# A graph kernel's gather passes: the order of their first steps, and when two blocks of table work are done

## The reference

```
h = x
for _ in range(2):                                   # two message passes
    e = concat(h[src], h[dst], edge_attr)            # 288 numbers an edge
    m = relu(e @ We1 + be1) @ We2 + be2
    h = h + segment_sum(m, dst)                      # sum over a node's incoming edges
x = layernorm(x + h + bias)
# then one graph convolution; each node also gets a further loop edge to itself, with w = 1
deg = segment_sum(w, dst);  dinv = 1/sqrt(deg), 0 where deg <= 0
g = relu(dinv * segment_sum(w * (dinv * (x @ W1.T))[src], dst) + bias1)
out = layernorm(x + (g + x))
```

## Time and profile before

| | |
|---|---|
| time, median of 3 runs | 2493.58 us (2489.06 to 2494.75) |
| the profiled execution: its own time, its span | 2492.94 us, 2491.1 us |
| PE busy, share of the span | 2223.8 us, 89% |
| POOL busy | 1747.1 us, 70% |
| DVE busy | 1524.0 us, 61% |
| ACT busy | 470.5 us, 19% |
| chain that ended last, largest line | POOL gat L523, 44% |

### The profile page before, as it was taken

The page is one execution under the profiler, slowest core; times in us unless marked ns, Lnnn a source line. Parts: engine busy times, 40 slices in busy tenths (PEclk is TensorE's granted clock), DMA queues, the critical chain, the costliest instruction groups (busy, mean ns, idle before and its releaser), DMA issues.

```text
span 2491.1 us, 49611 instructions
## 1 busy us (share of the span) xinstructions
PE 2223.8 (89%) x15066; PEld 1727.0 (69%) x15066; DVE 1524.0 (61%) x4032; ACT 470.5 (19%) x1057; POOL 1747.1 (70%) x1765
## 2 busy tenths in 40 slices
PE   2799999999999997899999999999998769999996
PEld 2576666666666666666666666666666669999995
DVE  2766666666666663465555555555554378777785
ACT  1211111111111111211111111111111133222322
POOL 2577777777777776377777777777777557777673
PEclk8899999999999995699999999999999579999998
DMA  5333333333333343333333333333333221111111
GB/s 125 81 100 99 100 99 100 99 100 99 100 100 100 99 99 97 87 81 99 100 98 99 99 95 98 98 98 99 100 98 92 66 64 50 50 50 50 46 49 50
DMA packets 156484, 218.67 MB, mean 88 GB/s; under 512 B 74232, under 2 KB 107887, under 8 KB 156276
## 3 DMA queue, kind: packets, MB, share of 16 engines
q0 software_dynamic: 56000, 114.80, 18.4%
q1 hardware_dynamic: 93236, 98.88, 14.7%
q10 hardware_dynamic: 7168, 4.09, 0.6%
HBM read 207.48 MB, written 10.12 MB: 87 GB/s over the span
## 4 chain that ended last, share of the span: by engine, by line
POOL 44%; issue 30%; PE 18%; DVE 3%; DMA 3%; POOLq 0%; ACT 0%; SPq 0%; DVEq 0%; ACTq 0%
POOL gat L523 44%; PE ps L708 6%; PE ps L699 6%; PE ps L593 3%; DMA gat<-dst_row 1%; PE ps L782 1%; DMA cbase_dram<-cint 1%; DMA gat<-z_dram,idx 1%; PE ps L778 1%; PE ps L651 1%; PE ps L611 1%; DVE node_a L1191 1%; DVE node_b L1097 0%; PE ps L627 0%; DVE node_b L1171 0%
## 5 line engine op out<-in xcount | busy, mean ns | idle before, releaser
L523 POOL DMA_INDIRECT gat<-p_dram,idx x1422 | 1418.2, 997 | 508.0 <-issue 450.3
L651 PE MATMUL ps<-node_a,x 128*128 128x512 bf16 x2400 | 739.6, 391 | 14.0 <-DVE node_a L1191 14.0
L593 PE MATMUL ps<-hot,msg 128*128 128x64 f32 x3232 | 425.4, 288 | 76.5 <-ACT msg L887 52.8
L1191 DVE TENSOR_SCALAR node_a<-ps,row_id 128x512 bf16<-128x512 f16 x1200 | 484.6, 467 | 8.4 <-PE ps L651 7.2
L593 PEld LDWEIGHTS ps<-hot,msg 128*128 128x128 f32 x3232 | 399.3, 201 | 97.8 <-ACT msg L887 63.0
L651 PE MATMUL ps<-node_a,adj 128*128 128x512 bf16 x1200 | 467.0, 389 | 0.0
L1153 DVE TENSOR_SCALAR lhs<-dbc,base_p 64x1024 f32<-64x1024 int32 x202 | 155.2, 768 | 477.2 <-DMA dbc<-dst_row 477.2
L583 PEld LDWEIGHTS ps<-rhs,lhs 96*128 96x128 f32 x3232 | 411.2, 200 | 44.1 <-DVE lhs L1153 15.6
L523 POOL DMA_INDIRECT gat<-z_dram,idx x328 | 318.9, 972 | 161.1 <-issue 98.4
L583 PE MATMUL ps<-rhs,lhs 96*128 96x128 f32 x3232 | 415.4, 284 | 14.6 <-DVE lhs L1153 10.8
L651 PEld LDWEIGHTS ps<-node_a,x 128*128 128x128 bf16 x2400 | 241.4, 104 | 269.0 <-issue 28.5
(11 more groups left out here) (146 smaller groups left out, 1650.2 us busy)
## 6 DMA issues: line engine op xcount, KB each, us to landing
dbc<-dst_row SPq DMA_DIRECT2D x202, 256.0 KB
lhs<-eaT SPq DMA_DIRECT2D x202, 128.0 KB
gat<-p_dram,idx POOLq DMA_INDIRECT x1422
rhs<-q_dram SPq DMA_DIRECT2D x202, 32.0 KB
gat<-z_dram,idx POOLq DMA_INDIRECT x328
idx<-src_g SPq DMA_DIRECT2D x243, 4.0 KB
p_dram<-node_a ACTq DMA_DIRECT2D x12, 256.0 KB, 3.4
q_dram<-node_b SPq DMA_DIRECT2D x12, 256.0 KB, 3.3
```

The lines of the kernel that those rows point to most:

```text
L523: return pool.indirect_dma_start(out=out_, out_offset=None, in_=table, in_offset=bass.IndirectOffsetOnAxis(ap=index, axis=0))
L593: last = nc.tensor.matmul(ps_agg(s), (msg if p < 2 else gat)[s][:, c, :], hot[s][:, c, (0 if p < 2 else 1), :], start=(c == 0), stop=(c == ...
L651: mm = nc.tensor.matmul(ps_own, p_part[k][:, t, :], shot[j % 2][:, t - t0, :, :].rearrange("p j e -> p (j e)"), start=(t == 0 and k == 0), ...
L1191: last = V.tensor_scalar(shot[j % 2][:, t - t0, :, :].rearrange("p j e -> p (j e)"), ps_ids, row_id[:, t:t + 1], None, ALU.is_equal)
```

## The change

In PE's steps 0 and 1 `products(g + 1)` is issued ahead of `own_part`. On DVE the first four `own_hots` calls move: those of parts 0 and 1 from the end of `table_parts` to the end of `vector_step(0)`, those of parts 2 and 3 from the middle of `vector_step(0)` and `vector_step(1)` to the end of `vector_step(1)`. `chunk_keys` and `join` move from the end of `vector_step(1)` to the end of `vector_step(95)` (`BATCHES` is 24).

```diff
                     def step(g, s, k, j, q):
+                        early_products = type(g) is int and g < 2
+                        if early_products:
+                            products(g + 1, 1 - s, k + s, (g + 2) % 4, (g + 2) // 4)
                         if q is not None:
                             own_part(j, q)
                         if type(g) is not int:
                             products(g + 1, 1 - s, k + s, (j + 1) % 4, q + 1 if j == 3 else q)
-                        elif g < NG - 1:
+                        elif g < NG - 1 and not early_products:
                             products(g + 1, 1 - s, k + s, (g + 2) % 4, (g + 2) // 4)
                         sums(g, s)
...
                         dve.wait_ge(part_left, base + 2 * len(QUADS))
                         dve.wait_ge(p_out, 16 * len(QUADS) * (p + 1))
-                        own_hots(0, 0)
-                        own_hots(1, 0)
-
...
                         if more:
                             one_hots(g + 1, 1 - s, k + s)
-                        if q is not None and j < 3:
+                        opening = type(g) is int and g < 2
+                        if opening:
+                            pass
+                        elif q is not None and j < 3:
                             own_hots(j + 1, q)
                         elif q is not None and not (type(q) is int and q == BATCHES - 1):
                             own_hots(0, q + 1)
...
                         if more:
                             scatter_hots(g + 1, 1 - s)
-                        if type(g) is int and g == 1:
+                        if opening:
+                            own_hots(2 * g, 0)
+                            own_hots(2 * g + 1, 0)
+                        if type(g) is int and g == 4 * BATCHES - 1:
                             (chunk_keys if p == 0 else join)()
```

## The result

The changed kernel takes 2498.38 us (median of 19 runs, 2491.36 to 2502.61), the kernel before, on the same chip and at the same time, 2491.88 us (2483.86 to 2497.16, 19 runs). The ratio is 1.0023, with a 95% interval of 1.0014 to 1.0033: 5.7 us more (3.5 to 8.2). The forecast's +3.9 lies inside that interval. The profiled execution took 2496.84 us, with a span of 2495.0 us. Lines of the kernel's file now stand three further down, except L1191.

What follows compares the result with a forecast made beforehand. POOL's gathers and the gaps between them, 74% of the span, bound the kernel. Pass 0 (+0.4 +1.65 +1.4 = +3.4) and pass 1 (-4.2 +0.8 +3.9 = +0.5) gave +3.9 on 2493.58: 2497.5 us, range 2489.5 to 2503.5.

Steps and rivals of the forecast that it cites:

- The gate: Ahead of group 4, the add of group 2 stands behind `own_hots(0, 1)`, awaiting turned ids: POOL waits about 11 and 4 us.
- The clock: PE's waits ahead of `own_part(2, 0)` halve its granted clock for a while: +1.65 us in pass 0, +0.8 in pass 1.
- The walk to group 4 in pass 0: DVE and PE followed in the new order, from DVE free at 77.94: group 4 starts at 112.7 against 112.28.
- The two walks: Both passes followed in the new order to group 4's start: 112.7 against 112.28, and 1087.7 against 1091.94.
- The tables: `chunk_keys` and `join` at step 95 slow POOL's gathers there: +1.4 us in pass 0, +3.9 in pass 1.
- the waits at group 4 would have swallowed them there: Left at their old place, the table work's gather delays, 1.4 and 3.9 us, would vanish in POOL's new waits.
- After group 4: one new stall and no second one: Add of group 3 follows group 2's within 6.9 us; POOL needs 9.0 for group 4: no further stall, 2 us in hand.
- The rival that the gate opens: `own_hots(0, 1)` done when POOL ends group 3, about 101 us: -13.6 us with the moved work, 2480.0; chance 0.10.

Runs made afterwards that it cites:

- join last: The changed kernel with `join` moved from the end of step 95 to the end of step 100; 2496.4 us, ratio 1.0012 to before.
- two inputs: The changed kernel plus one unused long DVE instruction, reading two SBUF operands, in each of steps 95 to 97 of pass 1; 2507.83 us, ratio 1.0068.
- one input: The changed kernel plus one unused long DVE reduction, reading one SBUF operand, in each of steps 95 to 97 of pass 1; 2500.85 us, ratio 1.0034.
- Steps only: The changed kernel with `chunk_keys` and `join` put back at the end of step 1; 2495.71 us, ratio 1.0023 to before.
- tables only: The kernel before with only `chunk_keys` and `join` moved from step 1 to step 95; 2490.25 us, ratio 1.000.
- the interleaved ones: The changed kernel with opening own one-hots spread one set a step, 2483.03 us; also with `join` at step 100, 2485.22, and further reordered, 2478.48.
- the last order: Changed kernel, own one-hots spread one set a step, `join` at step 100, next batch's first own one-hots behind the add in batch-ending steps; 2478.48 us, ratio 0.9952.

## Why the prediction was right

All five executions with the changed opening steps and the tables at step 95 or later (after, its repetition, join last, two inputs, one input; for the last row of the table the first two and one input) can be set against two of before. The times run from the start of POOL's first gather of a pass to the first of group 4, from there to the first of group 13, and from the first of group 95 to the end of the pass's last gather; means, us:

| | before | after | difference | forecast |
|---|---|---|---|---|
| pass 0, to group 4 | 56.4 | 57.3 | +0.9 | +0.4 and clock +1.65 |
| pass 0, groups 4 to 12 | 80.5 | 82.2 | +1.7 | 0 |
| pass 0, groups 95 to 100 | 56.3 | 56.9 | +0.6 | +1.4 |
| pass 1, to group 4 | 55.2 | 51.5 | -3.7 | -4.2 and clock +0.8 |
| pass 1, groups 4 to 12 | 81.2 | 83.9 | +2.7 | 0 |
| pass 1, groups 95 to 100 (`join` at step 95) | 55.9 | 58.4 | +2.5 | +3.9 |

They sum to +4.7; the ratio says +5.7. In the first and the third row the executions of the two kernels overlap (54.9 and 57.9 against 55.6 to 58.4; 56.1 and 56.5 against 56.1 to 57.3), so these two differences aren't clear of the spread. Groups 13 to 94 differ by less than the two executions of before do from each other (6.5 us in pass 1), so nothing is read from them.

- **The gate** was right in mechanism, place and size. The stall goes from group 2 to group 4, named by the add of group 2, 12.84 and 3.92 us against the forecast's about 11 and 4. PE's waits were 2.21 and 1.53 us against 2.1 and 1.5. Of POOL's old wait 2.14 us ahead of group 2 and 1.77 ahead of group 3 are left in pass 0, where the forecast had none. Moving that add ahead of the one-hots that need the turned ids gave 9 us by the ratios.
- **The clock**: right in pass 0, 1.64 us (5.53 less 3.89) against 1.65, in four of the five executions; in the fifth, two inputs, the part took 3.99 us behind the same wait. In pass 1 none of the five had a drop; the 0.8 taken as half a chance wasn't there. The walk to group 4 in pass 0 was a little too long elsewhere: it had +2.05 with the clock in it, and measured +0.9, with a base that moves by 3 us. Part of this is where it starts: DVE was free 1.6 us sooner behind the first gather than in the rows it was made from (77.15 less 55.20, against 77.94 less 54.41). The two walks have small slips in adding, without effect on the argument: 0.1 us in pass 0, and 0.2 in pass 1, where 1074.33, 0.68 and 2.49 make 1077.5 and not 1077.7.
- **The tables**: the mechanism was right, two terms were over-sized. And "the waits at group 4 would have swallowed them there" was wrong: with the tables left in step 1, group 4 started 2.6 and 0.9 us later, so the move also gives back up to 3.5 us, which the walk already had in it. `join` costs POOL 2.5 us, not 3.9; `chunk_keys` 0.6 by the table, not 1.4, and the seven gathers beside it took 7.9 us against 7.2 over that window of before. The error was to take the gather of 4.88 us near the start of pass 1 as `join`'s price at any place. Both gathers end 0.8 us behind `join`, but that one starts 0.38 us ahead of it, and the one of 3.29 at the end of the pass 1.21 us into it.
- **"After group 4: one new stall and no second one"** is the step that was mis-sized: it counted waits only, and in waits it held. But groups 4 to 12 take 4.4 us more in the two passes. Of it 1.35 is the gap of 1.65 us behind group 4's first gather in pass 1. The rest is in the gathers' own length: over 0.945 us a gather, the 63 gathers of groups 4 to 12 have 1.4 and 2.1 us in the two profiles of before, 3.3 to 3.7 in the five of after (pass 0); 2.0 and 2.9 against 3.2 to 4.4 in pass 1. Steps only has 2.7 and 1.6, tables only 2.5 and 2.4.

Which DVE instructions lengthen them the rows show. Over the two gather passes of all thirteen profiles 3,160 of 18,486 gathers took over 1.0 us. All but ten of these end 0.79 to 0.86 us (2,796) or 0.10 to 0.17 us (354) behind the end of a DVE instruction: 2,185 of them behind `one_hots`, 578 behind `hot`, 279 behind the cast of `hot`. POOL's gather of 112.66 starts with DVE's `hot` of 112.64 (L1050, two SBUF inputs) and takes 1.47 us; that of 118.25, 1.48, has another such `hot` at 118.23. Two rows of after's pass 1 show `one_hots`, to 1098.53, and the gather behind it, to 1099.35:

```profile
1097.78 0.75 DVE L1156 TENSOR_SCALAR lhs<-dbc,base_p 64x1024 f32<-64x1024 int32 x1
1097.89 1.46 POOL L523 DMA_INDIRECT gat<-p_dram,idx  x1 [0.30 <-issue]
```

In groups 4 to 12 of pass 0 `hot` costs the gathers 0.1 and 0.5 us in all in before's two profiles and 1.4 in each of after's five, `one_hots` 1.2 and 1.3 against 1.6 to 2.0. Why more of them meet after the change is only argued: a release by the add starts both engines at one moment, so their steps stay in phase for a while. No run moved `hot` alone, and steps only had the release with less of the length.

The late second gather came in every kernel where POOL had waited ahead of group 4 of pass 1, with 1.64 to 2.07 us, and in none where it hadn't (before, tables only, the interleaved ones); in pass 0 it came in none, behind waits of 5.61 to 14.41 us. What it waits for the profile doesn't show, and that stays open.

So the total was nearer than its parts, and that was luck: about 4.4 us were missing in groups 4 to 12, against 2.2 too much for the tables and 1.4 too much in the two walks with their clock.

The rival that the gate opens (2480.0) wasn't this kernel, but it is the one that the last order reaches: 2478.48 us, 12 us under before by its ratio, where the rival had 13.6.

## What to carry to other kernels

A stall that an edit takes away is worth only what the next gate on the same engine lets through: walk on to the next instruction that the engine must wait for, and ask what stands ahead of its releaser in the releaser's queue. An instruction that waits for a third engine shouldn't stand ahead of the one that frees the bounding engine; letting the add pass it turned 0.2% slower into 0.1% faster here. And take the base of such a walk from two or three executions: here one row of before moved by 3 us.

## What the hardware showed that I had not expected

- Two waits of PE at the same place, 2.21 and 1.53 us, left the granted clock at 0.50 for 3.1 us in pass 0 and at 1.00 in pass 1. Of the seven profiles with these two waits, the longer was followed by 0.50 in six and the shorter in one (steps only). Before, a wait of 1.14 us was followed by 0.50, so the length of the wait alone doesn't tell which it will be.
- A gather that a DVE instruction holds ends about 0.82 us behind that instruction, be it `hot` of 0.67 us, `one_hots` of 0.75 or `join` of 3.68, so what it loses is set by how far into the instruction it starts. `one_hots`, with one tensor from SBUF, holds it like those with two; the add, with one input from PSUM, doesn't, and beside a 3.48 us reduction the longest was 1.39.
- The gap of about 1.65 us between two gathers, with no releaser, in pass 1: in all seven profiles in which POOL had waited ahead of group 4 there, and in none of the six others.
